# A routed mixture-of-experts layer behind cross-attention: last normalisation, two scatter pairs and the late tables reordered, and the mean subtracted directly

## Chip, cores and metric

The kernel runs on one core of one Trainium2 chip. The metric is device time in microseconds of one execution. A core has TensorE (PE, with its weight loads PEld), VectorE (DVE), ScalarE (ACT), GpSimd (POOL) and the queue of SyncE (SP), each of which works through its own instructions in order; what one waits for from another is a semaphore.

## The reference, cut to what matters

Input `x` is 16 batches of 100 rows of 128 numbers; `ctx_1024` is 16 batches of 1444 rows of 128.

```
x = x + tanh(g_xattn) * xattn(layernorm(x), ctx, mask, w_input, dot_scale)
x = x + tanh(g_ffn)   * moe(layernorm(x), W_router, W_gate, W_up, W_down)

layernorm(x) = (x - mean) / sqrt(var + 1e-5)
xattn: att = in.w_input + (in * dot_scale) @ ctx^T - 1e30 * mask
       softmax(att) @ ctx
moe:   probs = softmax(x @ W_router^T) over 8 experts; the best 2, renormalised
       y_e   = (silu(x @ Wgate_e^T) * (x @ Wup_e^T)) @ Wdown_e^T      (F = 512)
       sum over the two chosen experts of weight * y_e
```

## The kernel before

**First stage, attention.** `step(b)` exists once for each engine and runs for b = 0 to 15. PE computes the scores of batch b (L1101), transposes the exponentials of batch b-1 (L1118), transposes the second normalisation of batch b-2 (`transpose_xn2`, L1137), computes its router logits (L1143) and multiplies the exponentials of b-1 with the context (L1129). DVE adds the attention result to x (`residual`, L798), takes mean and variance (`statistics2`, L805 and L808), subtracts the rounded from the exact weights (`split_weights`, L813), takes the masked maximum (L824), picks the two experts (`top_two`, `choose`) and, every second batch, works out the row numbers (`place`, L888). POOL makes 1/sqrt(var + eps) and the negative mean (`root1`, `root2`) and normalises (`normalise1`, `normalise2`, L554), and sends each batch's 200 rows (two copies of 100, one for each chosen expert) to the expert's region of the buffer `slots` in HBM with two indirect DMAs (`scatter`, L586).

**Second stage, experts.** The 3,200 rows lie sorted by expert in `slots` and are worked off in T = 32 tiles of 128 rows. The first EARLY = 8 tiles hold only rows of batches 0 to 9, which are certain early; tables that DVE computes say from which row a tile is read and which expert it takes: once for the first 8 tiles (`tile_counts`, `tile_runs`, `tile_rows`, `tile_experts` with False) and once for the other 24 (with True). SP loads a tile when its table is there (`load_rows`, L454): tiles 0 to 7 when all scatters of batches 0 to 9 have landed, tile 8 and the following when those of batches 10 to 15 have. After the load of tile 7 SP also issues eight writes of empty rows behind the regions (`clear_tail`, L458), and POOL waits for these (`tails_stored`) ahead of the scatter of batch 14.

For a tile k, PE transposes its rows (L1191), ACT rounds the transpose (`rowT_high`, L721), DVE takes the remainder (`rowT_low`, L1000), PE multiplies with gate and up weights (L1205 to L1207, `gate_up`), ACT takes silu (L732), DVE multiplies (L1022), PE transposes (`transpose_hidden`, L1216), ACT copies, PE multiplies with the down weights (`down`, L1232), ACT copies (L744) and POOL scatters the result (L642). There is one PSUM buffer for the row transposes, so `transpose_rows(k+1)` waits until `rowT_low(k)` is done. The steps overlap: `tile_step(i, k)` of PE runs `transpose_rows(k+1)`, `gate_up(k)`, `transpose_hidden(k-1)`, `down(k-2)`. The one exception is k = EARLY - 1 = 7: there `transpose_rows(8)` stands at the end of the step, behind `down(5)`, and `rowT_high`, `rowT_low` with it. Batches 14 and 15 are normalised, transposed and routed within steps 0 to 3 of this stage.

All order is written out by hand; there is no planner. POOL's order around the end of the first stage is: b = 15: normalise2(13), wait for the landing of batches 0 to 9, scatter 10; then normalise2(14), scatter 11, wait for landing, scatter 12, normalise2(15), wait for landing, scatter 13, `last_gates`, wait for the empty rows, and scatters 14 and 15 with a wait for landing ahead of each and behind the last. `pair_landed(late)` is that wait: for all scatters sent so far.

Of the kernel before, what the change touches and what calls it, by code (L numbers as in the profile page):

```python
# [47 lines left out]
EARLY = 8  # L48
# [6 lines left out]
def build(nc, x, ctx, ctx_cols, mask, w_input, w_small, w_experts, out):  # L55
# [43 lines left out]
    with ExitStack() as stack:  # L99
# [45 lines left out]
        back1 = sb("back1", [Q, B])  # L145
# [12 lines left out]
        back2 = sb("back2", [Q, 2])  # L158
# [100 lines left out]
        back1_done = sem("back1_done")  # L259
# [19 lines left out]
        back2_done = sem("back2_done")  # L279
# [208 lines left out]
        def _(pool):  # L488
# [7 lines left out]
            def root1(b0, b1):  # L496
                pool.wait_ge(mv1_done, b1)
                apart(pool)
                nc.gpsimd.tensor_scalar(var1[:, b0:b1], mv1[:, b0:b1, 1], EPS, None, ALU.add).then_inc(var1_done, b1 - b0)
                nc.gpsimd.tensor_scalar(back1[:, b0:b1], mv1[:, b0:b1, 0], -1.0, 0.0, ALU.mult, ALU.add).then_inc(back1_done, b1 - b0)  # L500
                pool.wait_ge(var1_done, b1)
                nc.gpsimd.tensor_tensor(rstd1[:, b0:b1], var1[:, b0:b1], power[:, 0:b1 - b0], ALU.pow).then_inc(rstd1_done, b1 - b0)

            def root2(b):
                s = b % 2
                pool.wait_ge(mv2_done, b + 1)
                apart(pool)
                nc.gpsimd.tensor_scalar(var2[:, s:s + 1], mv2[:, s, 1:2], EPS, None, ALU.add).then_inc(var2_done, 1)  # L508
                nc.gpsimd.tensor_scalar(back2[:, s:s + 1], mv2[:, s, 0:1], -1.0, 0.0, ALU.mult, ALU.add).then_inc(back2_done, 1)
                pool.wait_ge(var2_done, b + 1)  # L510
                nc.gpsimd.tensor_tensor(rstd2[:, s:s + 1], var2[:, s:s + 1], power[:, 0:1], ALU.pow).then_inc(rstd2_done, 1)
# [29 lines left out]
            def normalise1(b):  # L541
                s = b % 2
                pool.wait_ge(rstd1_done, b + 1)
                wait(pool, qT_raw, b - 1)
                wait(pool, input_dot_done, b - 1)
                pool.wait_ge(back1_done, b + 1)
                nc.gpsimd.tensor_scalar(xn[:, s, :], x_all[:, b, :], back1[:, b:b + 1], rstd1[:, b:b + 1],
                                        ALU.add, ALU.mult).then_inc(xn_done, 1)

            def normalise2(b):  # L550
                s = b % 2
                pool.wait_ge(rstd2_done, b + 1)
                pool.wait_ge(back2_done, b + 1)
                nc.gpsimd.tensor_scalar(pair_rows[:, b, :, 0:D], x_all[:, b, :].unsqueeze(1).to_broadcast([Q, 2, D]),  # L554
                                        back2[:, s:s + 1], rstd2[:, s:s + 1], ALU.add, ALU.mult).then_inc(xn2_done, 1)
# [49 lines left out]
            for b in range(B):  # L605
                if b >= 2:
                    root2(b - 2)
                    normalise2(b - 2)
                if b == B - 1:
                    pair_landed(0)  # L610
                if 5 <= b:
                    scatter(b - 5)
                if b == 2 or b == 6 or b == 10:
                    root1(b + 2, b + 6)
                if b + 2 < B:
                    normalise1(b + 2)
            root2(B - 2)
            normalise2(B - 2)
            scatter(11)
            pair_landed(1)  # L620
# [3 lines left out]
            pair_landed(1)  # L624
# [30 lines left out]
        def _(act):  # L655
# [67 lines left out]
            def tile_step(i, k):  # L723
                n = i * YRING + k
                if 0 < k and k + 1 < T and k != EARLY - 1:
                    rowT_high(i, k + 1)
# [18 lines left out]
                if k == EARLY - 1:  # L745
                    rowT_high(i, k + 1)
# [22 lines left out]
        def _(dve):  # L769
# [169 lines left out]
            def step(b):  # L939
                if b >= 2:  # L940
                    residual(b - 2)
                    statistics2(b - 2)
                if b >= 1:
                    attention_gain(b - 1)
                split = ROUNDED.get(b - 1, ())
                for c in split[:1]:
                    split_weights(c)
# [10 lines left out]
                if b == B - 1:  # L958
                    tile_experts(False)
                    for c in split[1:]:  # L960
                        split_weights(c)
# [10 lines left out]
                if b == 14:  # L972
                    tile_rows(False)
# [29 lines left out]
            def tile_step(i, k):  # L1003
                n = i * YRING + k
                if 0 < k and k + 1 < T and k != EARLY - 1:
                    rowT_low(i, k + 1)
# [20 lines left out]
                if k == EARLY - 1:  # L1027
                    rowT_low(i, k + 1)

            def between(n):  # L1030
                if n == 3:
                    tile_counts(True)
                if n == 4:
                    tile_runs(True)
                if n == 5:
                    tile_rows(True)
                if n == 6:
                    tile_experts(True)
# [34 lines left out]
        def _(pe):  # L1073
# [162 lines left out]
            def tile_step(i, k):  # L1236
# [3 lines left out]
                if 0 < k and k + 1 < T and k != EARLY - 1:  # L1240
                    transpose_rows(i, k + 1)
# [6 lines left out]
                if k == 2:  # L1248
                    transpose_xn2(B - 1)
                if 0 <= k - 1 < T:  # L1250
                    transpose_hidden(i, k - 1)
# [5 lines left out]
                if k == 3:  # L1257
                    ranks(LAST)
                if k - 2 >= 0:
                    down(i, k - 2, e)  # L1260
                if k == EARLY - 1:
# [56 lines left out]
```

## Time and profile before

| what | us |
|---|---|
| median of 3 runs | 255.49 |
| lowest and highest run | 253.91, 261.04 |
| the profiled execution | 254.09 |
| its span from first to last instruction | 252.3 |
| PE busy in the span | 222.3 |
| DVE, ACT, POOL busy | 137.9, 116.1, 112.7 |

The profiled execution lies 1.40 us under the median and 0.18 us over the lowest run. All starts below are counted from the start of the span. A line of the timeline gives the start, the duration, the engine, the line of the program, the operation, output and input, the count, and in brackets how long the engine sat idle before and what ended that. Ends of matmuls are modelled, so neighbours overlap by up to 0.16 us.

### The profile page before, as it was taken

The numbers are of one execution on the slowest core, as the hardware profiler recorded it, in microseconds if no ns is written. First come the engines' busy times: TensorE is split into PE (matmuls) and PEld (weight loads), VectorE is DVE, ScalarE is ACT, GpSimd is POOL, SyncE is SP. The second block draws the span as 40 slices with busy tenths as digits, with TensorE's granted clock in tenths as the row PEclk, the third lists the DMA queues.
The fourth block names the chain that finished last, engine by engine and source line by source line (L and its number), as shares of the span: only waits on it lengthen the run. The fifth ranks groups of instructions, "written<-read, shape, count | busy, mean of one in ns | idle before, by whom it ended". The sixth has DMA issues, their size and how long they took to land.

```text
span 252.3 us, 5442 instructions
## 1 busy us (share of the span) xinstructions
PE 222.3 (88%) x1431; PEld 175.7 (70%) x1432; DVE 137.9 (55%) x499; ACT 116.1 (46%) x270; POOL 112.7 (45%) x197
## 2 busy tenths in 40 slices
PE   7799999999999999988799899799999999999100
PEld 6377767786676867667488688688888888887000
DVE  4566556868778678676965366333344334332043
ACT  3173434563455645555474345345555454454000
POOL 3455331568645585456356755344432333333300
PEclk9999999999999999999999999999999999999855
DMA  6999999999879977958634501321211110000284
GB/s 184 322 404 270 359 270 314 306 303 260 304 277 250 353 249 221 274 173 263 246 83 141 183 19 40 84 66 64 55 42 45 52 43 31 21 21 34 60 221 130
DMA packets 19771, 44.38 MB, mean 176 GB/s; under 512 B 3690, under 2 KB 10134, under 8 KB 19734
## 3 DMA queue, kind: packets, MB, share of 16 engines
q1 hardware_dynamic: 16396, 39.26, 50.3%
q0 software_dynamic: 2560, 3.77, 4.6%
q10 hardware_dynamic: 790, 1.04, 1.6%
q8 instruction: 12, 0.20, 0.4%
q14 instruction: 13, 0.11, 0.1%
HBM read 37.71 MB, written 6.34 MB: 175 GB/s over the span
## 4 chain that ended last, share of the span: by engine, by line
PE 67%; DMA 8%; DVE 8%; issue 7%; POOL 6%; SPq 1%; ACT 1%; DVEq 0%; ACTq 0%; POOLq 0%
PE psum L1129 15%; PE psum L1232 11%; PE psum L1101 9%; PE psum L1205 6%; PE psum L1206 5%; PE psum L1207 5%; PE psum L1216 5%; PE psum L1118 4%; DMA ctxT<-in_ctx_cols 3%; DMA ctx_sb<-results 3%; POOL pair_rows L554 2%; PE psum L1091 2%; PE psum L1191 1%; POOL var L508 1%; PE psum L1137 1%
## 5 line engine op out<-in xcount | busy, mean ns | idle before, releaser
L642 POOL DMA_INDIRECT results<-y_sb,dest x32 | 30.7, 959 | 52.2 <-DVE dest L1011 26.0
L1129 PE MATMUL psum<-ctx_sb,probsT 128*100 128x128 f32 (+1 forms) x384 | 52.6, 281 | 0.0
L1129 PEld LDWEIGHTS psum<-ctx_sb,probsT 128*100 128x100 f32 (+1 forms) x384 | 43.8, 166 | 3.2 <-issue 0.2
L1022 DVE SCALAR_TENSOR_TENSOR scores<-probs,row_in,psum 128x512 f32<-128x512 f32 x32 | 23.9, 748 | 38.8 <-ACT probs L732 32.1
L1101 PE MATMUL psum<-ctxT,qT 128*100 128x512 f32 (+1 forms) x96 | 41.8, 571 | 1.1 <-DMA ctxT<-in_ctx_cols 1.1
L667 ACT ACTIVATE probsT<-psum 128x400 f32<-128x400 f32 x48 | 20.7, 505 | 42.0 <-PE psum L1118 41.9
L586 POOL DMA_INDIRECT slots<-pair_rows,slot_i x32 | 33.5, 1046 | 12.9 <-issue 6.3
L732 ACT ACTIVATE probs<-psum 128x512 f32<-128x512 f32 x32 | 19.1, 597 | 35.5 <-PE psum L1207 34.4
L1232 PE MATMUL psum<-w_down,hidT 128*128 x256 | 34.2, 276 | 0.4 <-issue 0.4
L1232 PEld LDWEIGHTS psum<-w_down,hidT 128*128 128x128 f32 x256 | 31.1, 192 | 0.8 <-issue 0.8
L1205 PE MATMUL psum<-w_hi,rowT_hi 128*128 x64 | 28.4, 443 | 1.7 <-issue 1.0
L1101 PEld LDWEIGHTS psum<-ctxT,qT 128*100 128x100 f32 x96 | 15.5, 166 | 19.9 <-issue 18.3
L696 ACT ACTIVATE probs<-scores,negmax 100x1444 f32<-100x1444 f32 x16 | 23.8, 1489 | 4.6 <-DVE negmax L831 4.5
L1206 PE MATMUL psum<-w_lo,rowT_hi 128*128 x64 | 25.3, 396 | 0.0
L1207 PE MATMUL psum<-w_hi,rowT_lo 128*128 x64 | 25.3, 395 | 0.0
L508 POOL TENSOR_SCALAR var<-mv 100x1 f32<-100x1 f32 x16 | 5.3, 331 | 42.7 <-DVE mv L808 42.5
L824 DVE CUSTOM_DVE_ANT_0 scores<-psum,zeros 100x1444 f32<-100x1444 f32 x11 | 18.3, 1661 | 7.5 <-PE psum L1101 7.4
L1118 PEld LDWEIGHTS psum<-identity,probs 100*128 100x128 f32 x192 | 17.6, 137 | 6.0 <-issue 5.7
L1216 PE MATMUL psum<-identity,scores 128*128 128x128 f32 x128 | 19.3, 273 | 0.1
L738 ACT ACTIVATE hidT<-psum 128x512 f32<-128x512 f32 x32 | 19.0, 593 | 0.5 <-PE psum L1216 0.5
L1118 PE MATMUL psum<-identity,probs 100*128 100x100 f32 x192 | 19.1, 249 | 0.0
L1216 PEld LDWEIGHTS psum<-identity,scores 128*128 128x128 f32 x128 | 15.8, 141 | 4.3 <-DVE scores L1022 0.3
(136 smaller groups left out, 304.3 us busy)
## 6 DMA issues: line engine op xcount, KB each, us to landing
ctxT<-in_ctx_cols SPq DMA_DIRECT2D x16, 722.0 KB, 8.6
ctx_sb<-in_ctx SPq DMA_DIRECT2D x16, 704.0 KB
w_raw<-in_w_experts SPq DMA_DIRECT2D x16, 256.0 KB
maskb<-mask_scaled SPq DMA_DIRECT2D x5, 541.5 KB
row_in<-slots SPq DMA_DIRECT2D x32, 65.0 KB
w_down<-in_w_experts SPq DMA_DIRECT2D x4, 512.0 KB
slots<-empty SPq DMA_DIRECT2D x8, 195.0 KB
ctx_sb<-results SPq DMA_DIRECT2D x4, 192.0 KB, 5.5
```

Of the source, the lines that this page charges most:

```text
L586: nc.gpsimd.indirect_dma_start(slots, bass.IndirectOffsetOnAxis(ap=slot_i[:, b, j:j + 1], axis=0), pair_rows[:, b, j, :], None).then_inc(s ...
L642: nc.gpsimd.indirect_dma_start(results, bass.IndirectOffsetOnAxis(ap=dest[:, s:s + 1], axis=0), y_sb[:, s, :], None).then_inc(y_stored[s], 16)
L696: nc.scalar.activation(probs[0:Q, :], scores[0:Q, :], ACT.Exp, bias=negmax[:, b % 2:b % 2 + 1], accum_out=rowsum[:, b % RING:b % RING + 1] ...
L1022: nc.vector.scalar_tensor_tensor(out=hidden[k % 2], in0=silu[k % 2], scalar=row_in[:, o, D:D + 1], in1=up_ps[k % 2], op0=ALU.mult, op1=ALU ...
L1101: last = nc.tensor.matmul(scores_home(b)[0:Q, n:n + m], qT[:, b % 2, :], ctxT[:, b % COL_RING, n:n + m], start=start, stop=stop)
L1118: last = nc.tensor.transpose(probsT_home(b, g)[0:rows[c], at:at + Q], probs[0:Q, starts[c]:starts[c] + rows[c]], identity[0:Q, 0:Q])
L1129: last = nc.tensor.matmul(attn_ps[0:Q, 0:D], probsT[0:rows[c], c, :], ctx_sb[0:rows[c], b % CTX_RING, c, :], start=(c == 0), stop=(c == CH ...
L1205: nc.tensor.matmul(ps, rowT_hi[:, o, :], hi, start=True, stop=False)
L1206: nc.tensor.matmul(ps, rowT_hi[:, o, :], lo, start=False, stop=False)
L1207: last = nc.tensor.matmul(ps, rowT_lo[:, o, :], hi, start=False, stop=True)
L1216: last = nc.tensor.transpose(hidT_ps[:, c * P:(c + 1) * P], hidden[k % 2][:, c * P:(c + 1) * P], identity[:, :])
L1232: last = nc.tensor.matmul(y_home(k), hidT[:, o, c * P:(c + 1) * P], w_down[:, bass.ds(e * F + c * P, P)], start=(c == 0), stop=(c == FC - 1))
```

## The change

- POOL's `back1` and `back2` (mean times -1) and their semaphores are gone; `normalise1` and `normalise2` take the mean itself and subtract it.
- POOL: within b = 15, behind scatter 10, come a wait for landing and scatter 11. After it: normalise2(14), scatter 12, normalise2(15), scatter 13, with no wait for landing between.
- DVE: `tile_rows(False)` goes from the end of step 14 to step 15, behind `statistics2(13)`; the last step's first `split_weights` goes behind the maximum and `tile_experts(False)`.
- DVE: of the late tables, `tile_runs(True)` moves from behind step 4 to behind step 3, `tile_rows(True)` from 5 to 4, `tile_experts(True)` from 6 to 5.
- PE: `ranks(LAST)` goes ahead of `transpose_hidden(2)` in step 3.
- PE, ACT, DVE: the exception for k = 7 now holds for k = 7 and k = 8: `transpose_rows(9)`, `rowT_high(9)` and `rowT_low(9)` also stand at the end of their step.

```diff
 def root1 / root2 (POOL)
-    nc.gpsimd.tensor_scalar(back1[:, b0:b1], mv1[:, b0:b1, 0], -1.0, 0.0, ALU.mult, ALU.add).then_inc(back1_done, ...)
-    nc.gpsimd.tensor_scalar(back2[:, s:s + 1], mv2[:, s, 0:1], -1.0, 0.0, ALU.mult, ALU.add).then_inc(back2_done, 1)
 def normalise2 (normalise1 alike)
-    pool.wait_ge(back2_done, b + 1)
     nc.gpsimd.tensor_scalar(pair_rows[:, b, :, 0:D], x_all[...],
-        back2[:, s:s + 1], rstd2[:, s:s + 1], ALU.add, ALU.mult).then_inc(xn2_done, 1)
+        mv2[:, s, 0:1], rstd2[:, s:s + 1], ALU.subtract, ALU.mult).then_inc(xn2_done, 1)
 POOL, for b in range(B)
     if 5 <= b:
         scatter(b - 5)
+    if b == B - 1:
+        pair_landed(1)
+        scatter(11)
 ...
 root2(B - 2)
 normalise2(B - 2)
-scatter(11)
-pair_landed(1)
 scatter(12)
 root2(B - 1)
 normalise2(B - 1)
-pair_landed(1)
 scatter(13)
 last_gates()
 DVE, step(b)
+    if b == B - 1:
+        tile_rows(False)
     if b >= 1:
         attention_gain(b - 1)
     split = ROUNDED.get(b - 1, ())
-    for c in split[:1]:
-        split_weights(c)
+    if b < B - 1:
+        for c in split[:1]:
+            split_weights(c)
     masked_max(b)
 ...
         tile_experts(False)
-        for c in split[1:]:
+        for c in split:
             split_weights(c)
 ...
-    if b == 14:
-        tile_rows(False)
 DVE, between(n)
     if n == 3:
         tile_counts(True)
+        tile_runs(True)
     if n == 4:
-        tile_runs(True)
+        tile_rows(True)
     if n == 5:
-        tile_rows(True)
-    if n == 6:
         tile_experts(True)
 PE, ACT and DVE, tile_step(i, k)
-    if 0 < k and k + 1 < T and k != EARLY - 1:
+    if 0 < k and k + 1 < T and k not in (EARLY - 1, EARLY):
         transpose_rows / rowT_high / rowT_low (i, k + 1)
 ...
+    if k == 3:                        # PE, ahead of transpose_hidden
+        ranks(LAST)
 ...
-    if k == EARLY - 1:
+    if k in (EARLY - 1, EARLY):
         transpose_rows / rowT_high / rowT_low (i, k + 1)
```

## Rows read from the trace of the kernel before

**Rows 1.** The page: busy time of each engine, and the chain of waits by engine.
```profile
PE 222.3 (88%) x1431; PEld 175.7 (70%) x1432; DVE 137.9 (55%) x499; ACT 116.1 (46%) x270; POOL 112.7 (45%) x197
PE 67%; DMA 8%; DVE 8%; issue 7%; POOL 6%; SPq 1%; ACT 1%; DVEq 0%; ACTq 0%; POOLq 0%
```
**Rows 2.** Busy time by stretch: start:end, length, each engine, granted clock, DMA.
```profile
157.80:160.00 2.20, 0.65 (x4) 0.28 (x2) 0.74 (x4) 0.72 (x3) 0.06 (x1) 1.00 0.35 90
...
200.00:229.00 29.00, 29.00 (x191) 25.39 (x191) 10.77 (x29) 15.15 (x39) 9.61 (x11) 1.00 0.10 32
```
**Rows 3.** Who waited for whom: total us, times, longest.
```profile
PE psum L1137 <- POOL pair_rows L554: 5.1, 7, 1.4
```
**Rows 4.** Timeline of PE, first stage: transposes of the normalised rows.
```profile
60.90 0.28 PE L1137 MATMUL psum<-identity,pair_rows 100*128 100x100 f32 x1 [0.55 <-POOL pair_rows L554]
...
92.52 0.28 PE L1137 MATMUL psum<-identity,pair_rows 100*128 100x100 f32 x1 [0.30 <-POOL pair_rows L554]
...
125.41 0.28 PE L1137 MATMUL psum<-identity,pair_rows 100*128 100x100 f32 x1 [1.42 <-POOL pair_rows L554]
```
**Rows 5.** Timeline of DVE and POOL at a long and a short negation.
```profile
58.82 0.68 DVE L813 TENSOR_TENSOR w_lo<-w_raw,w_hi 128x512 fp32r<-128x512 f32 x1
59.08 0.48 POOL L509 TENSOR_SCALAR back<-mv 100x1 f32<-100x1 f32 x1
59.52 0.56 POOL L511 TENSOR_TENSOR rstd<-var,power 100x1 f32<-100x1 f32 x1
...
106.70 0.19 POOL L509 TENSOR_SCALAR back<-mv 100x1 f32<-100x1 f32 x1
106.85 0.57 POOL L511 TENSOR_TENSOR rstd<-var,power 100x1 f32<-100x1 f32 x1
```
**Rows 6.** Timeline of DVE around its step 15.
```profile
119.44 0.19 DVE L888 TENSOR_TENSOR slot<-choice,psum 100x32 f32<-100x32 f32 x1 [1.99 <-PE psum L1156]
...
120.98 0.22 DVE L921 TENSOR_TENSOR reached<-tile_f,tile_end 100x64 f32<-100x64 f32 x1
...
122.09 0.35 DVE L798 SCALAR_TENSOR_TENSOR x_all<-psum,gain,x_all 100x128 f32<-100x128 f32 x1
...
128.85 0.35 DVE L798 SCALAR_TENSOR_TENSOR x_all<-psum,gain,x_all 100x128 f32<-100x128 f32 x1 [0.61 <-PE psum L1129]
```
**Rows 7.** Timeline of PE, second stage: batch 15, ranks, tiles 8 to 10.
```profile
140.33 0.28 PE L1137 MATMUL psum<-identity,pair_rows 100*128 100x100 f32 x1 [0.77 <-POOL pair_rows L554]
...
144.88 0.33 PE L1154 MATMUL psum<-chosen,before 100*100 100x24 f32 x2
...
157.82 0.33 PE L1191 MATMUL psum<-identity,row_in 128*128 128x128 f32 x1
159.13 0.30 PE L1191 MATMUL psum<-identity,row_in 128*128 128x128 f32 x1 [0.99 <-DVE rowT_lo L1000]
160.01 0.49 PE L1205 MATMUL psum<-w_hi,rowT_hi 128*128 x1 [0.58 <-issue]
...
162.84 0.27 PE L1191 MATMUL psum<-identity,row_in 128*128 128x128 f32 x1
```
**Rows 8.** Timeline of POOL from scatter 12 to the first result.
```profile
136.15 0.99 POOL L586 DMA_INDIRECT slots<-pair_rows,slot_i  x1 [1.78 <-DMA slots<-pair_rows,slot_i]
...
145.71 0.20 POOL L574 TENSOR_TENSOR pair_rows<-gate,ratio 100x2 f32<-100x2 f32 x1
146.82 1.10 POOL L586 DMA_INDIRECT slots<-pair_rows,slot_i  x1 [0.91 <-POOL pair_rows L574]
...
155.44 0.99 POOL L642 DMA_INDIRECT results<-y_sb,dest  x1 [2.25 <-DMA slots<-pair_rows,slot_i]
```
**Rows 9.** Timeline of SP's queue: loads of tiles, writes of empty rows.
```profile
125.29 8.67 SPq L454 DMA_DIRECT2D row_in<-slots  x8
134.74 8.78 SPq L458 DMA_DIRECT2D slots<-empty  x8
155.83 32.07 SPq L454 DMA_DIRECT2D row_in<-slots  x17
```

More of the change, by code:

```diff
@@ L144, in build @@
         mv1 = sb("mv1", [Q, B, 2])
-        back1 = sb("back1", [Q, B])
         var1 = sb("var1", [Q, B])
@@ L157, in build @@
         mv2 = sb("mv2", [Q, 2, 2])
-        back2 = sb("back2", [Q, 2])
         var2 = sb("var2", [Q, 2])
@@ L258, in build @@
         mv1_done = sem("mv1_done")
-        back1_done = sem("back1_done")
         var1_done = sem("var1_done")
@@ L278, in build @@
         mv2_done = sem("mv2_done")
-        back2_done = sem("back2_done")
         var2_done = sem("var2_done")
@@ L499, in root1 @@
                 nc.gpsimd.tensor_scalar(var1[:, b0:b1], mv1[:, b0:b1, 1], EPS, None, ALU.add).then_inc(var1_done, b1 - b0)
-                nc.gpsimd.tensor_scalar(back1[:, b0:b1], mv1[:, b0:b1, 0], -1.0, 0.0, ALU.mult, ALU.add).then_inc(back1_done, b1 - b0)
                 pool.wait_ge(var1_done, b1)
@@ L545, in normalise1 @@
                 wait(pool, input_dot_done, b - 1)
-                pool.wait_ge(back1_done, b + 1)
-                nc.gpsimd.tensor_scalar(xn[:, s, :], x_all[:, b, :], back1[:, b:b + 1], rstd1[:, b:b + 1],
-                                        ALU.add, ALU.mult).then_inc(xn_done, 1)
+                nc.gpsimd.tensor_scalar(xn[:, s, :], x_all[:, b, :], mv1[:, b, 0:1], rstd1[:, b:b + 1],
+                                        ALU.subtract, ALU.mult).then_inc(xn_done, 1)
             def normalise2(b):
@@ L1004, in tile_step @@
                 n = i * YRING + k
-                if 0 < k and k + 1 < T and k != EARLY - 1:
+                if 0 < k and k + 1 < T and k not in (EARLY - 1, EARLY):
                     rowT_low(i, k + 1)
@@ L1026, in tile_step @@
                     statistics2(B - 1)
-                if k == EARLY - 1:
+                if k in (EARLY - 1, EARLY):
                     rowT_low(i, k + 1)
@@ L1239, in tile_step @@
                     transpose_xn2(B - 2)
-                if 0 < k and k + 1 < T and k != EARLY - 1:
+                if 0 < k and k + 1 < T and k not in (EARLY - 1, EARLY):
                     transpose_rows(i, k + 1)
@@ L1256, in tile_step @@
                     pe.wait_ge(down_loaded, 16 * 4)
-                if k == 3:
-                    ranks(LAST)
                 if k - 2 >= 0:
                     down(i, k - 2, e)
-                if k == EARLY - 1:
+                if k in (EARLY - 1, EARLY):
                     transpose_rows(i, k + 1)
```

## The prediction

> **What bounds the kernel now.** I read the page first: PE is busy for 88% of the span and makes 67% of the chain that ended last, no other engine over 8% [rows 1]. So only what makes PE idle is worth anything, and the question at each part of the change is which PE gap it closes. The stretches say where gaps are: 29.00 of 29 us busy late in the second stage, but only 0.65 of 2.20 us between 157.80 and 160.00 [rows 2]. The list of waits gives the other place: seven waits of PE for POOL's second normalisation, 5.1 us in all, the longest 1.4 [rows 3]; six lie in the first stage, the seventh is batch 15's at 140.33 [rows 4, 7]. The change touches all of these, one part for each.
>
> **Part 1, the negation goes.** It stands between the variance and the root on POOL, ahead of the normalisation for which PE waits. A short one lasts 0.19 us and the root starts 0.15 after it; a long one lasts 0.48, and the root starts 0.44 after it [rows 5]. The long one lies in DVE's weight subtraction (58.82 to 59.50) and ends 0.06 behind it, so it was held and not working [rows 5]. If the root that moves into its place is held too, it ends only some 0.15 earlier; if not, 0.44 earlier. I take 0.15: the row at 59.08 shows a POOL operation held by just this neighbour. The Trainium skill (GPSIMD Engine Reference, Specifications) states that GpSimd shares its SBUF interfaces with VectorE and contends with a DVE instruction with two SBUF inputs. By that rule the root is held as well and the sum stays at 0.15 a wait; without it this part would be worth 0.9 more. The subtraction itself replaces an addition of the same shape; POOL subtracts nowhere in the trace, so I bound it by nothing and by 0.34, what the root (0.57) lasts over a plain column operation (0.23), and take nothing.
>
> Five of the six first-stage waits lie ahead of step 15. Four give 0.15 each; the one at 92.52 has a negation of `root1` in its path too and gives its whole 0.30. Together 0.90. In the first four steps PE never waits for POOL, so nothing comes there.
>
> **Part 2, step 15 on DVE.** `tile_rows(False)` (120.98 to 122.1, 1.1 us) stands ahead of `residual(13)`, and PE's 1.42 us wait at 125.41 hangs on that residual [rows 4, 6]. Moved behind it, PE's wait nearly goes. But DVE works without a gap from 119.44 until it idles 0.61 ahead of the next residual at 128.85 [rows 6], and this residual, the statistics and `rowT_low(0)` behind it set when the first expert tile can start. Its work in the step is only reordered (the weight split too), so DVE can give back those 0.61 us and no more. Gain 0.60, the rest of PE's wait returns as a wait for `rowT_low(0)`. What the later table could delay is the load of tile 0 at 125.29, which waits for the scatters of batches 0 to 9; the table would be there at 123.2, and still is not last. Tile 0 takes some 2 us to be read (as tile 8: issued 155.83, transposed 157.82 [rows 7, 9]) and is there when PE comes, within 0.1 us, ahead of the 0.6 that PE has over DVE.
>
> **Part 3, batch 15 earlier.** POOL's scatter 12 waited 1.78 us at 136.15 and stood ahead of batch 15's normalisation; PE then waited 0.77 at 140.33 [rows 7, 8]. New order, in shifted times: scatter 10 at 124.6; its landing 2.5 to 3.0 us after its second DMA begins (0.99 issue plus 1.78 or 2.25 idle less 0.25 of restart [rows 8]), so scatter 11 at 128.5 to 129.2; normalise2(14) done by 132.7 to 133.2, wanted at 133.5; scatter 12; normalise2(15) done by 136.8 to 137.3, wanted at 138.0. So the 0.77 goes, with at least 0.3 to spare. PE now stands 0.90 + 0.60 + 0.77 = 2.27 us earlier. `ranks(LAST)` is another half microsecond earlier (it swaps with four transposes); the late tables follow it and come one step sooner. On DVE, `tile_runs` (1.0 us) is now ahead of `rowT_low(5)` and `tile_rows` (1.5) ahead of `rowT_low(6)`; each has 0.8 to 1.0 us before PE needs it, so I cost that at nothing, with 0.3 as its upper bound.
>
> **Part 4, when tile 8 can be read.** It needs the landing of scatter 15, which stands behind scatter 14 at 146.82. That one started 0.91 after the last gate operation was over [rows 8]; no row says what ended these 0.91. It also waits for the eight writes of empty rows, the last issued at 134.74 + 8.78 = 143.52 [rows 9]. These hang on SP, whose chain starts with the load of tile 0 and moves by 0.75 only, to 142.77. POOL's gates move by at least 2.27 and would allow 143.6 + 0.9. So the empty rows become the later of the two. Their landing takes between 1.99 (a tile's load) and 3.0 us (a scatter) [rows 7 to 9], so with 0.25 for the restart scatter 14 starts at 145.0 to 146.0; had they been the releaser before, at 146.82 - 0.75 = 146.07. I take 145.5. The Trainium skill (DMA: Bandwidth & Descriptors, Anatomy of one DMA) has a fit of 2.0 us plus bytes over 436e3 for one DMA, most of it the receipt of the write; for 195 KB that is an estimate of 2.45 us, so scatter 14 would start at 145.5 by it too, and a time below the bound of 145.0 is unlikely by that rule.
>
> From scatter 14 to the transpose of tile 8 the trace has 157.82 - 146.82 = 11.00 us, so that comes at 156.5 (156.0 to 157.1). PE would be there at 157.82 - 2.27 = 155.55: it waits 0.95 us. Most of part 3's gain is lost here.
>
> **Part 5, tile 9's transpose.** Before, tile 8's products started 2.19 after its transpose: 1.31 for rounding and remainder until tile 9 was transposed, then 0.88 until the products [rows 7]. With tile 9 out of the way they start at 1.31. But the exception now holds for step 8 also: tile 9 is transposed 2.83 later (160.01 to 162.84 [rows 7]), and nothing lies between it and its own products, so the full 2.19 comes once more, where before the products of tile 9 followed at 162.87 without a gap. New start of tile 9's products: 156.5 + 1.31 + 2.83 + 2.19 = 162.8. The part removes 0.88 and adds 2.19: a loss of 1.3.
>
> **The sum.** 162.87 before, 162.8 after: -0.1 us, bounds -0.6 and +0.5 by the time of scatter 14. Behind it PE is busy without a gap and then the tail follows unchanged [rows 2], so the end moves by the same. 254.09 - 0.1 = 254.0 for an execution like the profiled one. The median of the runs shown is 1.40 above that execution and the lowest run just under it; I add 0.3 for a median and say 254.3.
>
> **The rivals.**
> Tile 8 in time: the empty rows land early or never counted, and scatter 14 follows the gates. Tile 8 is transposed at 155.55, tile 9's products start at 161.9: -1.0, 253.4 as a median. For: the 0.91 of idle shows that something other than the gates ended before, and it may be gone. Against: the 3.30 us between 143.52 and 146.82 are not much more than a landing.
> The second gap does not come: PE's instruction stream has the tile number and the products ready and restarts at 0.4 or less behind the last remainder, or tile 9 is transposed while `down(6)` runs. Then part 5 gains 0.9 and part of the 2.19 stays out: -1.5 to -2.2, 252.5. Against: exactly this order gave 2.19 at tile 8.
> Slower: SP's chain does not move. It starts when the scatters of batch 9 have landed, which share the queues with the down weights; if those are bound by bandwidth rather than by their issue, the empty rows end as before, scatter 14 starts at 146.8, tile 9's products at 164.1: +1.3, 255.6. It decides once scatter 14 starts later than 145.6. For: seven us pass from the issue of batch 9's second copy to its landing at 125. Against: the queues were idle before the down weights were issued, so issue sets them.
> The roots are not held: part 1 is worth 0.9 more, all of PE's and SP's times move by it: 253.4.
>
> **How the numbers follow.** Forecast 0.42; tile 8 in time 0.17; no second gap 0.12; slower 0.20; roots not held 0.09. The cases lie between 252.5 and 255.6, all within 2% (5.1 us, about what a measurement of this kernel can tell from no change), and the runs of before scatter by more than they differ, from 253.91 up. Range 252.1 to 256.4. Faster by over 2% needs 250.4, which no case reaches: 0.04 for what I don't see. Slower by over 2% needs 260.6: 0.03. Within: 0.93.
>
> **What would show it.** In the profile after: part 1, the root 0.15 behind its old distance from the variance also inside DVE's weight subtraction; part 2, the wait for the transpose in step 15 down to some 0.2 and a wait for `rowT_low(0)` of about 1 in its stead; part 3, no wait at batch 15's transpose; part 4, SP's last empty write at about 142.8, scatter 14 at about 145.5, and PE idle about 1 us ahead of tile 8's transpose; part 5, two gaps of PE, 1 us and more at tile 8's products and 2 us at tile 9's. I am wrong if scatter 14 comes under 144.5, or if tile 9's products follow its transpose by less than 1.3.

## The result: 3.4% slower, and where the time went

The changed kernel took 263.89 us in the median (262.32 to 264.58, 6 runs) against 254.94 (253.91 to 261.04, 6 runs) of the kernel before on the same chip: a ratio of 1.0339, 95% interval [1.0271, 1.0406]. The prediction was 254.3, with 0.03 on slower. It was wrong. The profiled execution took 262.32 us, with a span of 260.5 (before: 254.09 and 252.3). Some executions of a kernel fall into a slower state, and a ratio compares only those outside it, so it need not be the quotient of the two medians beside it.

Line numbers of the kernel after are some 8 lower: the second normalisation is L546 (L554 before), the first L540 (L547), the transpose that waits for it L1129 (L1137), scatters L578, the products' first line L1197, a tile's transpose L1183. First the page after, engines and chain of waits, which answers to [rows 1]:
```profile
PE 225.6 (87%) x1431; PEld 177.0 (68%) x1432; DVE 138.5 (53%) x499; ACT 116.8 (45%) x270; POOL 126.2 (48%) x176
PE 62%; DVE 11%; POOL 10%; issue 8%; DMA 4%; ACT 1%; DVEq 1%; ACTq 1%; POOLq 0%
```
POOL is busy 13.5 us longer than before although 21 of its instructions are gone (197 to 176), and its share of the chain rises from 6 to 10%. Instructions fewer, busy time more: some operation has become slower. The view of one source line (duration in ns: min/median/max) names it, first after, then before:
```profile
L546 POOL TENSOR_SCALAR pair_rows<-x_all,mv,rstd x16: 1231/1239/1244, 23.5 to 144.3; 100x256 f32<-100x256 f32 x16
L540 POOL TENSOR_SCALAR xn<-x_all,mv,rstd x16: 782/804/1320, 5.8 to 117.2; 100x128 f32<-100x128 f32 x16
```
```profile
L554 POOL TENSOR_SCALAR pair_rows<-x_all,back,rstd x16: 557/558/568, 21.5 to 139.6; 100x256 f32<-100x256 f32 x16
L547 POOL TENSOR_SCALAR xn<-x_all,back,rstd x16: 437/450/505, 6.0 to 110.8; 100x128 f32<-100x128 f32 x16
```
The subtraction costs 0.68 us more at 256 columns and 0.35 at 128, so 2.7 ns a column. The second normalisation is what PE waits for; the waits, which answer to [rows 3]:
```profile
PE psum L1129 <- POOL pair_rows L546: 7.8, 9, 1.4
PE psum L1183 <- DMA row_in<-slots: 2.3, 1, 2.3
```
PE in the second stage after, which answers to [rows 7]: batch 13's transposed rows, the first expert products, batch 15's rows, then tile 8's transpose, its products, tile 9, tile 10 and tile 9's products.
```profile
131.59 0.28 PE L1129 MATMUL psum<-identity,pair_rows 100*128 100x100 f32 x1 [0.49 <-POOL pair_rows L546]
...
137.04 0.50 PE L1197 MATMUL psum<-w_hi,rowT_hi 128*128 x1 [0.54 <-DVE rowT_lo L993]
...
145.71 0.28 PE L1129 MATMUL psum<-identity,pair_rows 100*128 100x100 f32 x1
...
165.71 0.33 PE L1183 MATMUL psum<-identity,row_in 128*128 128x128 f32 x1 [2.30 <-DMA row_in<-slots]
166.82 0.49 PE L1197 MATMUL psum<-w_hi,rowT_hi 128*128 x1 [0.78 <-DVE rowT_lo L993]
...
169.64 0.27 PE L1183 MATMUL psum<-identity,row_in 128*128 128x128 f32 x1
170.80 0.30 PE L1183 MATMUL psum<-identity,row_in 128*128 128x128 f32 x1 [0.89 <-DVE rowT_lo L993]
171.67 0.49 PE L1197 MATMUL psum<-w_hi,rowT_hi 128*128 x1 [0.57 <-issue]
```
I cut every profiled execution at the same five events of PE: the scores of batch 2 (19.58 before, 21.85 after), batch 13's transpose, the first expert products, tile 8's transpose and tile 11's (165.68 and 174.50). Lengths in us, each a difference of two starts on PE's timeline:

```
                                  start  stage 1  to first  to tile 8  8 to 11
before                            19.58  105.83     5.23      27.18      7.86
after                             21.85  109.74     5.45      28.67      8.79
e1  subtraction only              19.97  112.04     6.89      32.63      9.22
e4  copy, then subtraction        21.70  112.70     5.22      29.44      9.24
e7  subtraction in second only    21.44  113.53     5.22      29.38      9.23
e8  subtraction in first only     20.20  105.96     6.80      27.54      9.44
e3  no negation, mean added       19.44  104.87     6.88      28.50      9.27
e2  order only                    21.41  104.62     6.00      27.74     10.33
e5  order, tile 8 alone           21.84  104.80     6.00      27.94      9.05
e6  e5, empty rows after tile 3   19.83  104.26     6.02      29.83      7.70
e10 before, empty rows after 5    21.13  105.21     5.23      28.54      7.66
e11 before, ten forms at the end  19.86  104.97     5.22      28.65      7.66
e9  e5, empty rows after 5        21.41  103.57     6.01      26.05      7.70
e13 the same again                21.50  104.74     6.01      25.85      7.75
e12 e9, exception for 8 and 9     20.20  104.94     6.00      25.86      8.97
```
Of the 8.82 us by which tile 11 is later after the change, 2.27 lie ahead of batch 2, 3.91 in the first stage, 0.22 up to the first products, 1.49 up to tile 8 and 0.93 behind it. The 2.27 at the start are not the change's: starts of 19.4 to 21.8 come with and without the subtraction (e2 and e13 have none), so one profiled execution can be over 2 us off there. Over these stages e11 is the same program as the kernel before, and e10 is up to the load of tile 5: the three differ by 0.86 in the first stage, and before and e11 by 1.47 up to tile 8. A difference of that size between two rows says nothing by itself.

### The profile page after: what moved, and what is told of

Read it like the earlier page. It is cut to its first block, busy times and chain, and to the rows that moved or that the text cites. A ratio compares the mean times of both kernels' runs of the same rounds, so it can differ in the third digit from the quotient of the medians.

```text
span 260.5 us, 5388 instructions
## 1 busy us (share of the span) xinstructions
PE 225.6 (87%) x1431; PEld 177.0 (68%) x1432; DVE 138.5 (53%) x499; ACT 116.8 (45%) x270; POOL 126.2 (48%) x176
## 4 chain that ended last, share of the span: by engine, by line
PE 62%; DVE 11%; POOL 10%; issue 8%; DMA 4%; ACT 1%; DVEq 1%; ACTq 1%; POOLq 0%
PE psum L1121 13%; PE psum L1224 10%; PE psum L1197 7%; PE psum L1093 6%; PE psum L1199 6%; PE psum L1198 6%; PE psum L1208 5%; POOL pair_rows L546 4%; DMA ctx_sb<-results 3%; POOL rstd L505 2%; PE psum L1110 2%; PE psum L1083 2%; PE psum L1129 1%; PE psum L1183 1%; POOL xn L540 1%
## 5 line engine op out<-in xcount | busy, mean ns | idle before, releaser
L1093 PE MATMUL psum<-ctxT,qT 128*100 128x512 f32 (+1 forms) x96 | 42.7, 582 | 0.0
L578 POOL DMA_INDIRECT slots<-pair_rows,slot_i x32 | 33.8, 1056 | 15.1 <-issue 7.7
L1197 PE MATMUL psum<-w_hi,rowT_hi 128*128 x64 | 28.4, 443 | 2.6 <-DVE rowT_lo L993 1.3
L503 POOL TENSOR_SCALAR var<-mv 100x1 f32<-100x1 f32 x16 | 4.1, 259 | 35.4 <-DVE mv L800 35.3
L546 POOL TENSOR_SCALAR pair_rows<-x_all,mv,rstd 100x256 f32<-100x256 f32 x16 | 19.8, 1238 | 1.7
```

Of the source, the lines that this page charges most:

```text
L578: nc.gpsimd.indirect_dma_start(slots, bass.IndirectOffsetOnAxis(ap=slot_i[:, b, j:j + 1], axis=0), pair_rows[:, b, j, :], None).then_inc(s ...
L1093: last = nc.tensor.matmul(scores_home(b)[0:Q, n:n + m], qT[:, b % 2, :], ctxT[:, b % COL_RING, n:n + m], start=start, stop=stop)
L1197: nc.tensor.matmul(ps, rowT_hi[:, o, :], hi, start=True, stop=False)
```

## Experiments

All times are medians beside the kernel before on the same chip. The runs of before scatter from 252.1 to 262.4, so what is under 1% is read from the stages above rather than from medians.

**e1 and e2: the change in two halves.** e1 is the kernel before with part 1 alone, e2 the changed kernel with the negation and the addition put back.
```
e1: - back = mean * -1; (x + back) * rstd      e2: after, with
    + (x - mean) * rstd                            (x + back) * rstd again
```


> The kernel before with part 1 alone: no negation, the mean is subtracted; all orders as before. Theory S (the subtraction on GpSimd is slow by itself and sits in PE's path): the normalisation of 256 columns lasts 1.24 us in place of 0.56 and that of 128 columns 0.80 in place of 0.45; each of the 6 to 9 waits of PE grows by 0.5 (0.68 less the 0.15 that the negation gives back), the start of the kernel is 2 us late, the span grows by 6 to 8 us. Rival O (the new order of scatters, tables and tile 9 costs the time): within 1 us of before.

Measured: 268.16 against 256.82, ratio 1.0459 [1.0377, 1.0542]. L546 lasts 1238 ns. PE's waits for it:
```profile
PE psum L1129 <- POOL pair_rows L546: 13.7, 10, 3.6
```
The cause is the one of theory S. The size is larger (11.3 us by the medians, not 6 to 8), and the kernel does not start late (19.97 in the table). Part of the surplus is clock: the granted clock of TensorE is 0.75 from batch 13's transpose to the first products and 0.90 from there to tile 8, and 1.00 over both in the kernels before and after (last section).

> The changed kernel with the negation and the addition put back; all its new orders stay. Theory S: within 1 us of before; my sum gave -0.1 (-0.6 to +0.5), with two gaps of PE at tiles 8 and 9 and scatter 14 at 145 to 146. Rival O: 5 us or more slower than before, near the changed kernel.

Measured: 257.15, ratio 1.0021 [0.9986, 1.0056], no difference. The whole loss lies in part 1, and the order alone changes nothing measurable. With the subtraction in place the new order seems to help: the changed kernel is 3.4% slower, e1 4.6%, and PE's waits for the second normalisation are 7.8 us against 13.7. The two intervals touch, so how much it helps is not shown. The normalisation lasts 558 ns in e2.

**e3 and e4: the operation or its operand?** e3 drops the negation but adds the mean (it normalises other numbers); e4 keeps an extra operation, a copy of the mean, and subtracts the copy.
```
e3: (x + mean) * rstd                 e4: back = mean * 1; (x - back) * rstd
```


> The kernel before without the negation, but the mean is added where it must be subtracted, so the numbers normalised are others; operands and instruction count are those of the changed kernel, only the operation is not. If the operation (subtract) is what is slow: 0.56 us for 256 columns, and the whole is 0.5 to 1.2 us faster than before. If the operand (a column out of a pair in place of a dense one) is slow: 1.24 us as in the changed kernel, and 6 us slower.

Measured: 257.14 (251.43 to 259.58, 4 runs), too scattered to tell the 0.5 to 1.2 us of the forecast from nothing. With the same operand `mv` as the change, but an addition:
```profile
L546 POOL TENSOR_SCALAR pair_rows<-x_all,mv,rstd x16: 553/554/559, 21.1 to 140.6; 100x256 f32<-100x256 f32 x16
```


> The kernel before with the negation turned into a copy (times 1) and the dense copy subtracted: the instruction count and operands are those of before, only the operation differs. If the operation is slow: 1.24 us for 256 columns and 7 to 9 us slower than before, a little more than with the subtraction alone. If the operand is: 0.56 and the time of before.

Measured: 266.87 (263.55 to 270.14, 4 runs), some 10 us over the 256.82 of before, where 7 to 9 were forecast. With the same operands and instructions as before, but a subtraction:
```profile
L554 POOL TENSOR_SCALAR pair_rows<-x_all,back,rstd x16: 1229/1238/1242, 23.5 to 149.3; 100x256 f32<-100x256 f32 x16
```
It is the operation. Reading `mv` in place of a dense column costs nothing, and the removed negation doesn't matter beside it.

**e7 and e8: which of the two subtractions.** Part 1 for the second normalisation alone, and for the first alone.
```
e7: first (x + back1) * rstd1, second (x - mean2) * rstd2
e8: first (x - mean1) * rstd1, second (x + back2) * rstd2
```


> The kernel before with only the second normalisation changed: it subtracts the mean (100 x 256 elements), and its negation is gone; the first normalisation keeps negation and addition. My theory: the second normalisation costs 0.68 us more and is what PE waits for, from about the third batch on at every batch, so this half carries nearly the whole loss of the run with part 1 alone: 8 to 11 us, ratio 1.030 to 1.043, and PE's waits for it come to 10 us and more. Rival, that GpSimd's total time is what counts (both halves add to its queue): the loss splits as the added time, 0.68 to 0.35, so 7.5 here and 4 in the other half.

Measured: 267.61 (263.79 to 270.96, 4 runs) against 256.42 (lowest 253.56): 11.2 us by the medians and 10.2 by the lowest runs.
```profile
PE psum L1133 <- POOL pair_rows L550: 12.6, 11, 2.8
```


> The kernel before with only the first normalisation changed: it subtracts the mean (100 x 128 elements, 0.35 us longer each), and its negation is gone; the second keeps negation and addition. My theory: it runs two batches ahead of need, behind the operations that PE waits for, so only the stages at the start and what it holds up on GpSimd's queue pay: under 2 us, ratio 1.000 to 1.008, PE's waits for the second normalisation within 1.5 us of the 5.1 in the kernel before. Rival, GpSimd's total time counts: 3.5 to 4.5 us slower, ratio 1.014 to 1.018.

Measured: 258.37, ratio 1.0063 [1.0007, 1.0119], and PE's waits at 6.0, both within the forecast.
```profile
PE psum L1133 <- POOL pair_rows L550: 6.0, 7, 1.8
```
16 times 0.68 and 16 times 0.35 are 10.9 and 5.6 us of POOL's time. In the first stage the one costs 7.70 us and the other 0.13 (table; 8.56 and 0.99 if e11 stands for before). So POOL's total time doesn't set the loss, but what stands between a batch's statistics and PE's transpose; the first normalisation runs behind the operation that PE waits for. What e8 loses besides, 1.57 up to the first products and 1.58 behind tile 8, lies in two stages with a lower granted clock (0.75 and 0.82).

**e11: ten forms side by side.** Added at the end of GpSimd's program, with the mean, the root or both as per-partition values.
```
+ (x + mean) * root, (x - mean) * root, x * root + mean, x * root - mean,
+ x + mean, x - mean, (x + mean) * root, (x - mean) * root, x + x, x - x
```


> The kernel before with ten operations more at the end of GpSimd's program, after its last results have landed, all 100 x 256 elements of fp32, with the same broadcast input as the second normalisation: add then multiply, subtract then multiply, multiply then add, multiply then subtract, add alone, subtract alone, then the first two once more, and an addition and a subtraction of two tensors. My theory, that it is the subtraction of a per-partition value that is slow on GpSimd, wherever it stands: 0.55 for add-multiply and multiply-add, 1.24 for both orders with a subtraction, and the subtraction alone above the addition alone by some 0.6. Rival, that only the pair subtract then multiply is slow (a form without a fast path): multiply then subtract and the subtraction alone take 0.55 or less. For two tensors I expect no difference between the two, with no row to go by.

GpSimd's timeline there, neighbours in one row; "x2" is the sum of two:
```profile
238.35 1.78 POOL L665 TENSOR_SCALAR pair_rows<-xn,mv,rstd 100x256 f32<-100x256 f32 x2 [1.49 <-DMA results<-y_sb,dest]
240.13 1.76 POOL L665 TENSOR_SCALAR pair_rows<-xn,rstd,mv 100x256 f32<-100x256 f32 x2
...
246.51 0.61 POOL L666 TENSOR_TENSOR pair_rows<-xn 100x256 f32<-100x256 f32 x1
247.08 1.06 POOL L667 TENSOR_TENSOR pair_rows<-xn 100x256 f32<-100x256 f32 x1
```
The second pair by itself (min and max are its two operations):
```profile
L665 POOL TENSOR_SCALAR pair_rows<-xn,rstd,mv x2: 552/888/1223, 240.1 to 240.7; 100x256 f32<-100x256 f32 x2
```
It starts at 240.1 and its second member at 240.7, so multiply-add is the 0.55 and multiply-subtract the 1.22: the place of the subtraction makes no difference. The forms behind these run beside DVE's additions of two SBUF tensors (241.29 to 243.41, 244.84 to 246.41 and, below, from 246.82 on), and can't be compared with each other. The first pair once more:
```profile
244.25 2.30 POOL L665 TENSOR_SCALAR pair_rows<-xn,mv,rstd 100x256 f32<-100x256 f32 x2
```
```profile
246.82 2.47 DVE L1071 TENSOR_TENSOR x_all<-x_all,ctx_sb 100x512 f32<-100x512 f32 x3 [0.41 <-DMA ctx_sb<-results]
```
Its addition lasts 0.54 and its subtraction, beside DVE, 1.76 in place of 1.24. The lone addition lasted 1.46 beside DVE, the lone subtraction 0.92 with DVE idle for all but its first 0.08. The subtraction of two tensors (1.06) lies wholly within DVE's additions and the addition (0.61) about half, so whether the two differ between tensors is not shown.

**e5, e6, e9, e10: the order, and when the empty rows go out.** e2 already showed the order at no gain, and its trace why: the empty rows released scatter 14 (POOL, then SP's queue and PE, of e2).
```profile
144.93 0.19 POOL L574 TENSOR_TENSOR pair_rows<-gate,ratio 100x2 f32<-100x2 f32 x1
147.34 1.10 POOL L586 DMA_INDIRECT slots<-pair_rows,slot_i  x1 [2.21 <-DMA slots<-empty]
```
```profile
136.51 8.27 SPq L458 DMA_DIRECT2D slots<-empty  x8
```
```profile
159.77 0.33 PE L1191 MATMUL psum<-identity,row_in 128*128 128x128 f32 x1 [1.73 <-DMA row_in<-slots]
```
e5 is e2 with the exception for tile 8 alone.
```
- if 0 < k and k + 1 < T and k not in (EARLY - 1, EARLY):
+ if 0 < k and k + 1 < T and k != EARLY - 1:
- if k in (EARLY - 1, EARLY):
+ if k == EARLY - 1:
```


> The order of the change with negation and addition kept (as in the earlier run of the order alone), but the exception for the transpose at the end of a step holds again for tile 8 alone. My theory, that the exception for tile 9 costs a second gap of PE: in the run with the order alone tile 9's products started 1.98 us after tile 9's transpose; here they follow it without a gap over 0.6, and the time is 1.3 to 2.0 us under that run, 0.992 to 0.997 of the kernel before. Rival, that this gap only takes the place of one further on, or that other gaps open as PE comes sooner: no difference to the order alone, ratio 1.000 to 1.003. The wait of tile 8's transpose for its rows stays in both at 1.5 to 2 us.

Measured: 256.79, ratio 1.0051 [1.0009, 1.0093]: no gain, against my theory. The second gap is gone and tiles 8 to 11 take 9.05 instead of 10.33, but PE's clock had fallen in both behind the wait for tile 8 (in e2 it was 0.66 from 160 to 165). Stretches (start:end, length, busy time of PE, PEld, DVE, ACT, POOL, granted clock, DMA share, GB/s) of e5:
```profile
155.00:160.00 5.00, 3.92 (x29) 3.40 (x27) 1.57 (x3) 2.62 (x6) 2.39 (x3) 1.00 0.14 33
160.00:165.00 5.00, 3.06 (x8) 2.23 (x9) 0.65 (x3) 0.56 (x2) 2.48 (x3) 0.72 0.31 95
```
A product there lasts 0.63 instead of 0.40. That is worth 1.3 us (9.05 against 7.70 in e9): a gap of PE can cost more than its own length.

e6 is e5 with the writes of empty rows after the load of tile 3.
```
- if n == EARLY - 1:      (after tile 7)
+ if n == 3:
    sp.wait_ge(tails_ready, 1); clear_tail(e) for all e
```


> The kernel of the previous expectation, and beside it SyncE issues the eight writes of empty rows after the load of tile 3 in place of tile 7, some 4 us sooner. My theory, that in the new order the landing of the empty rows sets scatter 14: it now starts when the last gate operation is over, 1.5 to 3 us sooner against the rows around it, its wait for the empty rows is gone, tile 8's transpose no longer waits for its rows (under 0.5 where the order alone had 1.73), and the time is another 1.2 to 2.0 us lower, 0.985 to 0.991 of the kernel before. Rival, that scatter 14 is set by the gates or by GpSimd's own time within 0.5 us anyway: the wait for the rows stays over 1.2, and the time is that of the previous kernel within 0.5 us. A second rival, the loads of tiles 4 to 7, now behind these writes on the queue, come late and PE waits for them in their turn: no gain or a loss of up to 1 us.

Measured: 255.99, ratio 1.0005 [0.9959, 1.0052]. The second rival was right: tile 8's wait is gone, and tile 4, whose load is now queued behind the eight writes, makes PE wait instead.
```profile
142.74 0.33 PE L1191 MATMUL psum<-identity,row_in 128*128 128x128 f32 x1 [2.20 <-DMA row_in<-slots]
```
Scatter 14 does not come sooner either:
```profile
148.35 1.10 POOL L586 DMA_INDIRECT slots<-pair_rows,slot_i  x1 [5.15 <-DVE slot_i L892]
```
It waits for the row numbers `slot_i` of batches 14 and 15, which DVE works out from PE's `ranks(LAST)`, and in step 3 that stands behind tile 4's transpose.

e9 puts them after the load of tile 5 (`if n == 5`).

> The order of the change with negation and addition kept, the exception at the end of a step for tile 8 alone, and SyncE issues the writes of empty rows after the load of tile 5 (tile 7 in the change, tile 3 in the last try, where the load of tile 4 came 2.2 us late). My theory: the empty rows are over some 2.3 us sooner, scatter 14 starts that much sooner (2.0 to 2.5 us after the last gate operation is over turns into 0.9 to 1.2), tile 8's transpose waits under 0.5 us for its rows, no other load is late, and the time is 1.5 to 2.5 us under the order alone: ratio to the kernel before 0.990 to 0.996. Rival, that PE loses in other waits what it wins here, or that runs differ by more than that: 0.998 to 1.004. Second rival, a load of tile 6 or 7 is late in its turn: a wait for rows of over 1 us, ratio over 1.000.

Measured: 252.11 against 256.77, ratio 0.9893 [0.9828, 0.9958]. Scatter 14 starts 0.97 after the gates, and tile 8's transpose waits for nothing:
```profile
144.25 0.19 POOL L574 TENSOR_TENSOR pair_rows<-gate,ratio 100x2 f32<-100x2 f32 x1
145.41 1.10 POOL L586 DMA_INDIRECT slots<-pair_rows,slot_i  x1 [0.97 <-DVE slot_i L892]
```
```profile
157.04 0.27 PE L1191 MATMUL psum<-identity,row_in 128*128 128x128 f32 x1
158.16 0.30 PE L1191 MATMUL psum<-identity,row_in 128*128 128x128 f32 x1 [0.84 <-DVE rowT_lo L1001]
159.07 0.49 PE L1205 MATMUL psum<-w_hi,rowT_hi 128*128 x1 [0.61 <-issue]
```
The ratio of e9 lies just below the forecast of 0.990 to 0.996. e10 does the same to the kernel before.

> The kernel before with one thing changed: the writes of empty rows go out after the load of tile 5 in place of tile 7. My theory: in the kernel before, GpSimd's gates and the empty rows end at nearly the same time (0.91 us between the last gate operation and scatter 14), so this alone wins at most 0.6 us, ratio 0.997 to 1.000. Rival, that the empty rows alone held scatter 14 also there, by more than the 0.91: tile 8's wait shrinks by 1 us and more, ratio 0.993 to 0.996.

Measured: 257.61, ratio 1.0011 [0.9944, 1.0077]. Scatter 14 starts 1.26 after the last gate operation and 0.92 after `slot_i`, so it was not the gates that set it, though my theory said so; the time fits the forecast, nothing won. Without the new order, earlier empty rows are worth nothing measurable, and without earlier empty rows the new order is worth nothing (e5, 1.0051). Together they win 1%.

**e12 and e13: the second exception, and the best kernel again.** e12 is e9 with the exception for tiles 8 and 9, as the change has it; e13 is e9 on this chip.

> The order with the writes of empty rows after tile 5's load, and here the exception at the end of a step for tiles 8 and 9, as the change has it. My theory: from tile 8's transpose to tile 11's it takes 8.8 us (7.70 in the run with the exception for tile 8 alone), since tile 9's products start 2.0 us behind its transpose, so 1.1 us slower than the next kernel of this call: ratio to the kernel before 0.993 to 0.998. Rival, that the earlier start of tile 8's products gives back as much (0.88): within 0.3 us of it.

> The kernel that was fastest so far (order of the change, negation and addition kept, empty rows after tile 5's load, exception for tile 8 alone), once more on this chip. My theory: ratio to the kernel before 0.986 to 0.994, a gain of 1.5 to 3.5 us that is real and not the chip's. Rival, that the 0.989 was luck of six runs: 0.996 to 1.003.

Measured on one chip with before at 255.86: e12 254.49, ratio 0.9971 [0.993, 1.0012]; e13 252.84, ratio 0.9875 [0.9819, 0.9932], both within the forecast. In e13 the empty rows still end the wait of scatter 14, 1.41 after the gates, where e9 had 0.97. Tile 9's exception costs 1.65 us by the medians and 1.22 by the traces (8.97 against 7.75). PE of e12 at tiles 8 to 10:
```profile
158.11 0.50 PE L1205 MATMUL psum<-w_hi,rowT_hi 128*128 x1 [0.84 <-DVE rowT_lo L1001]
160.95 0.27 PE L1191 MATMUL psum<-identity,row_in 128*128 128x128 f32 x1
162.28 0.30 PE L1191 MATMUL psum<-identity,row_in 128*128 128x128 f32 x1 [1.05 <-DVE rowT_lo L1001]
163.14 0.49 PE L1205 MATMUL psum<-w_hi,rowT_hi 128*128 x1 [0.56 <-issue]
```
The kernel e9/e13 (parts 2 and 3 of the change, the empty rows two loads sooner, parts 1 and 5 left out) beats both the kernel before and the changed one.

## Why the prediction was wrong

**Part 1 is the step that failed**, in one term: "The subtraction itself replaces an addition of the same shape; POOL subtracts nowhere in the trace, so I bound it by nothing and by 0.34 [...] and take nothing." It costs 0.68. The upper bound came from another comparison (a root against a plain operation, one column), which has no bearing on what 256 columns cost. It was charged to no path and was not even carried into the range: 0.34 at each of PE's seven waits alone would have been 2.4 us, and a price per column could not be excluded by any row. The second normalisation stands between statistics and PE's transpose at every batch. Where it was changed alone (e7), the first stage takes 113.53 us in place of 105.83: PE's waits for it there are 9.9 us in place of 4.4, and PE is busy 103.59 in place of 101.48, at a granted clock of 0.98 in place of 1.00. Neither of the two signs of being wrong that the prediction names came up (scatter 14 under 144.5, tile 9's products within 1.3 of its transpose): both lie in other parts than the one that failed.

The rest of part 1 was right. The root that moved into the negation's place is held up by DVE's weight subtraction too (DVE, then POOL, after):
```profile
112.05 0.68 DVE L805 TENSOR_TENSOR w_lo<-w_raw,w_hi 128x512 fp32r<-128x512 f32 x1
```
```profile
112.00 0.24 POOL L503 TENSOR_SCALAR var<-mv 100x1 f32<-100x1 f32 x1 [3.08 <-DVE mv L800]
112.32 0.85 POOL L505 TENSOR_TENSOR rstd<-var,power 100x1 f32<-100x1 f32 x1
113.27 1.24 POOL L546 TENSOR_SCALAR pair_rows<-x_all,mv,rstd 100x256 f32<-100x256 f32 x1
```
It lasts 0.85 instead of 0.57 and ends 1.17 behind the start of the variance, where before, with the negation, it was 1.31 (58.77 to 60.08): 0.14 saved, 0.15 forecast. The rule in the Trainium skill on which this was weighed (GPSIMD Engine Reference, Specifications: shared SBUF interfaces, contention with a DVE instruction of two SBUF inputs) agrees with this row, and with the lone addition in e11, which took 1.46 where addition and multiplication together take 0.55 with DVE idle. Whether the 0.90 of the sum came is not shown. In e3, where the negation is gone and nothing is subtracted, the first stage is 0.96 shorter than before's, but only 0.10 shorter than e11's. Up to the first products e3 then takes 1.65 longer (6.88 against 5.23), at a granted clock of 0.75 (last section).

**Part 2** was right in kind: PE's 1.42 at batch 13 becomes 0.49 (after) or none (e2), DVE's idle 0.61 is gone, and a wait for `rowT_lo` of 0.54 stands ahead of the first products. From batch 2 to the first products the order gains 0.44 in e2 and 0.31 in e13, 1.48 in e9, for a forecast of 0.60. But e10 and e11, with the old order, need 0.62 and 0.87 less than before too, so the 0.60 is not shown.

**Part 3** was right in kind: no wait at 145.71 after, nor in e2. From the first products to tile 3's (137.04 to 148.37 after, 130.64 to 142.82 before) it takes 0.85 less; the forecast was 0.77. The term itself varies: batch 15's wait is 1.26 in e10 and 1.09 in e11, and the same stretch takes 10.95 and 10.98 in e2 and e5 against 12.18, 12.67 and 12.50 in before, e10 and e11, so 1.2 to 1.7 less.

**Part 4** had the releaser of scatter 14 right. After and before, POOL from the last gate operation to the first result, which answers to [rows 8], and SP's queue, to [rows 9]:
```profile
150.69 0.20 POOL L566 TENSOR_TENSOR pair_rows<-gate,ratio 100x2 f32<-100x2 f32 x1
153.62 1.11 POOL L578 DMA_INDIRECT slots<-pair_rows,slot_i  x1 [2.73 <-DMA slots<-empty]
...
158.85 0.99 POOL L578 DMA_INDIRECT slots<-pair_rows,slot_i  x1 [2.82 <-DVE dest L1004]
...
163.36 0.99 POOL L634 DMA_INDIRECT results<-y_sb,dest  x1 [2.23 <-DMA slots<-pair_rows,slot_i]
```
```profile
142.87 8.18 SPq L454 DMA_DIRECT2D slots<-empty  x8
```
The last empty write is issued at 151.05 and scatter 14 starts 2.57 later (2.56 in e2); the sum had 2.7 (145.5 less 142.8). By the fit in the Trainium skill (DMA: Bandwidth & Descriptors, Anatomy of one DMA) the landing is an estimate of 2.45 ahead of the restart. With the 0.25 for the restart, that agrees with these rows within 0.15; e13 has 3.02. The Trainium skill states the fit for a DMA that GpSimd issues, and these are issued by SyncE, so it is the figure of a near case. Scatter 14 comes 16.58 after the first products, forecast 16.4; it is 16.64 in e5 and 15.31 in e2, since SP's last empty write, counted from the scores of batch 2, ends 1.5 us later in e5 than in e2, with nothing changed ahead of it.

The 0.91 ahead of scatter 14 that the prediction could put down to nothing was the wait for the row numbers. In the kernel before DVE ends them at 145.90:
```profile
145.71 0.19 DVE L892 TENSOR_REDUCE slot_i<-slot 100x4 uint32<-100x32 f32 x1
```
Scatter 14 starts 0.92 later, and the same 0.92 or 0.93 stands between the two in ten of the other traces. It is longer only in after, e2, e5 and e13, where the empty rows come last. So not the gates but the row numbers were the other releaser; the sum didn't hang on it.

What was too small is the stretch from scatter 14 to tile 8's transpose: taken over as 11.00, it is 12.09 after and 12.43 in e2, because the idle time ahead of scatter 15 is 2.82 and 2.88, not the 1.70 of the kernel before (the row above names DVE for it, but the program has nothing there but the wait for landing). So PE waits 2.30 and 1.73, not 0.95. The 11.00 was one execution's: e11, the same program as before there, has 3.03 ahead of scatter 15, 12.33 for the stretch and a wait of 1.32 for tile 8's rows. Why a scatter lands 1.1 us later in some runs is not settled: the idle time is 1.70 in e4, e6, e7, e8, e9, e12 and e13, 2.08 in e5, 2.67 in e10, 2.96 in e3 and 3.08 in e1.

**Part 5** was right: tile 9's products follow its transpose by 2.03, forecast 2.19, and the part costs 1.22 to 1.65 (e12 against e13), forecast 1.3.

Without the subtraction the sum of -0.1 us stands beside e2's ratio of 1.0021. That fits, but it proves less than it seems: e2 has none of part 1's 0.90 either, its interval reaches from -0.4 to +1.4 us, and its trace has two things that the sum had not, a longer wait at tile 8 and a fall of the clock behind it. What is shown is that the other parts together cost next to nothing and that the one operation new to the trace decided the case. Of the rivals none had it; the slower one was about SP's queue, not about POOL's own speed.

## What to carry to other kernels

An arithmetic operation that an engine does nowhere in the trace has no price there; bound it in proportion to its size on every path where it stands, and give the upper bound a rival of its own, above all if the same row already limits the busiest engine. Two changes that are each worth nothing can be worth a per cent together (e5, e10, e9), since each brings forward one of two releasers of the same instruction: the order the row numbers, the early writes the empty rows. A term read from one execution has that execution's luck in it: a second trace of the kernel before would have shown 12.33 in place of 11.00. Before a write is moved up in a queue, look at which load behind it has the least slack: two places too early (e6), it takes back what it won.

## What was not expected of the hardware

On GpSimd a subtraction of fp32 with a per-partition value is slower than an addition: 1.24 against 0.56 us at 100 x 256 and 0.80 against 0.45 at 100 x 128, in either order with a multiplication.

Granted clock: behind a wait for tile 8 it was 0.72 in e5 (PE busy 3.92 of 5 us ahead), so part of the stretch ran at 1.2 in place of 2.4 GHz, and 1.00 after, where PE had been busy 3.41 of the 5 us ahead and waited longer (2.30):
```profile
160.00:165.00 5.00, 3.41 (x25) 2.91 (x23) 1.56 (x3) 2.12 (x5) 2.33 (x3) 1.00 0.13 33
165.00:170.00 5.00, 3.43 (x20) 2.68 (x20) 1.10 (x3) 1.48 (x4) 2.53 (x3) 1.00 0.34 96
```
The table's last column gives the price. With the exception for tile 8 alone the stretch takes 7.66 to 7.86 at full clock (before, e6, e9, e10, e11, e13), 9.05 in e5 and 9.22 to 9.44 in e1, e3, e4, e7 and e8, which all show a granted clock of 0.66 or 0.67 over the 5 us behind tile 8's products. The column "to first" has it too: 5.22 or 5.23 with the old order at full clock, 6.80 to 6.89 in e1, e3 and e8. Here is that stretch of e3:
```profile
124.31:131.19 6.88, 6.55 (x44) 6.16 (x45) 4.00 (x23) 3.34 (x8) 2.57 (x4) 0.75 0.29 73
```
So the same kind of gap can cost 1.2 to 1.8 us more or not. The length of the one wait ahead doesn't decide it. Tile 8's transpose had waited at most 0.13 in e4, e7 and e8, where the clock fell, and 1.03, 1.32 and 2.30 in e10, e11 and after, where it held. Batch 13's transpose had waited 1.60 in e3, where it fell, and 2.13 in e7, where it held. The runs here don't say when.
